# Last layer of a four-layer graph kernel: three rounded passes in place of full float32 products

## The reference, cut to what matters

```python
def _L3_gnn_ref(base_features, neighbor_mask, parent_child_mask, Wq, ..., alpha, gamma):
    x = base_features                      # 8192 x 256
    Q = x @ Wq + bq                        # 256 -> 128
    K = x @ Wk + bk
    V = x @ Wv + bv
    scores = einsum(Q, K) * scale + parent_child_mask * alpha, masked by neighbor_mask
    attn_out = einsum(softmax(scores), V)  # 64 x 64 per graph
    refined = attn_out @ Wo + bo + x       # 128 -> 256
    child_sum = einsum('nm,bmd->bnd', parent_child_mask, refined)
    ...
```

## Time and profile before

| | |
|---|---|
| median of 3 runs | 2340.16 us (2339.61 to 2341.25) |
| the profiled execution: its own time | 2342.6 us |
| its span, first to last instruction | 2340.7 us |
| PE busy | 2172.1 us, 93% of the span |
| DVE, ACT, POOL busy | 1391.9, 1206.5, 480.1 us |
| mean granted TensorE clock | 0.981 of full speed |

### The profile page before, as it was taken

One profiled execution on the slowest core, in us unless ns is written; L12 is line 12 of the kernel. 1 busy time (PEld: TensorE's weight loads), 2 busy tenths in 40 slices (PEclk: granted clock), 3 DMA queues, 4 the chain that ended last, 5 costly groups with the idle time before them and its releaser, 6 DMA issues. The chain is left out here.

```text
span 2340.7 us, 39332 instructions
## 1 busy us (share of the span) xinstructions
PE 2172.1 (93%) x14671; PEld 1939.7 (83%) x14671; DVE 1391.9 (59%) x2733; ACT 1206.5 (52%) x2295; POOL 480.1 (21%) x905
## 2 busy tenths in 40 slices
PE   5999999999969989999999999999998897979997
PEld 3888888888859988888888889988887897968886
DVE  3788778877855645443334433444433787857776
ACT  1453455345523347644444434444433566958887
POOL 3344334433430000000000000000000221016665
PEclk9999999999979999999999999999999898989999
DMA  2110111011122101000000000000000331012221
GB/s 97 33 55 18 40 49 54 18 40 49 37 82 63 54 30 36 1 18 1 1 1 19 19 1 1 1 1 1 1 1 18 107 109 54 0 32 64 72 72 50
DMA packets 76397, 81.77 MB, mean 35 GB/s; under 512 B 6545, under 2 KB 74001, under 8 KB 75409
## 3 DMA queue, kind: packets, MB, share of 16 engines
q1 hardware_dynamic: 76304, 80.51, 10.9%
HBM read 55.33 MB, written 25.17 MB: 34 GB/s over the span
## 5 line engine op out<-in xcount | busy, mean ns | idle before, releaser
L298 PE MATMUL ps<-R 128*128 128x256 f32 (+3 forms) x8520 | 1490.9, 335 | 38.2 <-DVE R L1506 14.2
L298 PEld LDWEIGHTS ps<-R 128*128 128x128 f32 x8520 | 1326.6, 190 | 183.2 <-DVE R L767 14.8
L1200 ACT ACTIVATE late_half<-ps,lstm_bias 128x512 f32<-128x512 f32 (+2 forms) x460 | 283.0, 669 | 383.0 <-PE ps L298 382.9
L340 POOL TENSOR_TENSOR ln_veps<-ln_mv,eps_tile 128x2 f32<-128x2 f32 x128 | 28.4, 222 | 1283.0 <-DVE ln_mv L323 1283.0
L829 PE MATMUL ps<-H 128*128 128x256 f32 x1024 | 237.6, 381 | 3.0 <-ACT H L750 1.7
L829 PEld LDWEIGHTS ps<-H 128*128 128x128 f32 x1024 | 189.0, 191 | 26.1 <-ACT H L750 1.9
L1235 DVE TENSOR_TENSOR late_half<-late_half 128x1024 f32<-128x1024 f32 (+2 forms) x32 | 37.6, 1175 | 186.8 <-ACT late_half L1200 186.8
L1197 ACT ACTIVATE late_half<-late_half 128x1024 f32<-128x1024 f32 (+2 forms) x66 | 68.1, 1031 | 124.4 <-DVE late_half L1240 78.4
L1237 DVE TENSOR_TENSOR late_half<-late_half 128x1024 f32<-128x1024 f32 (+2 forms) x32 | 37.6, 1175 | 132.6 <-ACT late_half L1200 132.6
L366 DVE SCALAR_TENSOR_TENSOR H<-H,ln_rstd 128x256 f32<-128x256 f32 x192 | 106.5, 596 | 6.7 <-POOL ln_rstd L333 3.2
L319 DVE BATCH_NORM_STATS2 ln_stats<-H 128x6 f32<-128x256 f32 x256 | 95.9, 416 | 5.3 <-POOL H L711 2.0
(11 more groups left out here) (208 smaller groups left out, 2860.6 us busy)
## 6 DMA issues: line engine op xcount, KB each, us to landing
H<-in_x SPq DMA_DIRECT2D x64, 256.0 KB, 4.1
residual<-H SPq DMA_DIRECT2D x32, 256.0 KB, 2.2
H<-residual SPq DMA_DIRECT2D x32, 256.0 KB, 2.9
arena<-residual SPq DMA_DIRECT2D x32, 256.0 KB, 2.7
residual<-arena SPq DMA_DIRECT2D x32, 256.0 KB, 2.2
H_state<-residual SPq DMA_DIRECT2D x32, 256.0 KB, 2.7
out<-H_state SPq DMA_DIRECT2D x32, 256.0 KB, 2.2
arena<-in_wih SPq DMA_DIRECT2D x4, 1024.0 KB, 5.0
```

What stands on the lines that cost most here:

```text
L298: mm = pe.matmul(out, lhsT(a), rhs(b), start=start and n == 0, stop=stop and n == len(PASSES) - 1)
L1200: ins = act.activation(into[q][:, m, 0:x.cols], gate_ps(q, m, x.cols), ACT.Tanh if q == TANH_G else ACT.Sigmoid, bias=lstm_bias[:, x.p - 1 ...
```

## The change

The query, key, value and output products of the last layer are issued through `exact_mm`, 12, 12 and 6 rounded passes in place of 4, 4 and 2 float32 products. Their inputs are split in two parts: ACT writes the rounded part where it wrote the copy (slots 3 and 10), and DVE, in two new slots 3 and 10, writes the rest. The weights are split once by GpSimd, during the third layer's second product. The ticks of the plan are set anew: PE's slots 4 to 12, ACT's 4 to 13, DVE's 6 to 12, POOL's 11 and 12 and SP's 13 move by one or two; the period and the leads stay.

```diff
         @block.gpsimd
         def _(pool):
+            pool.wait_ge(l3_loaded, 5 * 16)
+            for n, (split, w) in enumerate(splits3):
+                pool.tensor_scalar(split[:, 0], w, 1.0, None, ALU.mult).then_inc(w3_hi, 1)
+                pool.wait_ge(w3_hi, n + 1)
+                pool.tensor_tensor(split[:, 1], w, raw(split[:, 0]), ALU.subtract)
...
     plan4 = dict(
         period=34, lead=(0, 8, 17, 26),
-        pe={1: 19, 3: 28, 4: 30, 5: 32, 6: 35, 9: 42, 10: 44, 11: 46, 12: 48},
-        act={0: 8, 2: 27, 3: 29, 4: 34, 5: 38, 7: 38, 9: 43, 10: 45, 11: 48, 13: 57},
-        dve={1: 23, 6: 35, 8: 42, 11: 47, 12: 51},
-        pool={1: 23, 3: 28, 11: 48, 12: 51},
-        sp={10: 33, 13: 57})
+        pe={1: 19, 3: 28, 4: 31, 5: 33, 6: 36, 9: 43, 10: 45, 11: 48, 12: 50},
+        act={0: 8, 2: 27, 3: 29, 4: 35, 5: 39, 7: 39, 9: 44, 10: 46, 11: 50, 13: 59},
+        dve={1: 23, 3: 30, 6: 36, 8: 43, 10: 47, 11: 49, 12: 53},
+        pool={1: 23, 3: 28, 11: 50, 12: 53},
+        sp={10: 33, 13: 59})
...
-                    act.activation(xT3_f[s], feature_major(s, 1), ACT.Copy).then_inc(xT3_ready[s], 1)
+                    act.activation(xT3_r[s][:, 0], feature_major(s, 1), ACT.Copy).then_inc(xT3_hi[s], 1)
...
-                    act.activation(atT3[s], token_major(s, 1, P), ACT.Identity, bias=bv3_col[:, 0:1])\
-                       .then_inc(o3T_ready[s], 1)
+                    act.activation(oT3_r[s][:, 0], token_major(s, 1, P), ACT.Identity, bias=bv3_col[:, 0:1])\
+                       .then_inc(o3T_hi[s], 1)
...
+                if slot == 3:
+                    dve.wait_ge(xT3_hi[s], turn + 1)
+                    dve.tensor_tensor(xT3_r[s][:, 1], feature_major(s, 1), raw(xT3_r[s][:, 0]), ALU.subtract)\
+                       .then_inc(xT3_ready[s], 1)
+                if slot == 10:
+                    dve.wait_ge(o3T_hi[s], turn + 1)
+                    dve.scalar_tensor_tensor(out=oT3_r[s][:, 1], in0=token_major(s, 1, P), scalar=bv3_col[:, 0:1],
+                                             in1=raw(oT3_r[s][:, 0]), op0=ALU.add, op1=ALU.subtract)\
+                       .then_inc(o3T_ready[s], 1)
...
-            pe.wait_ge(l3_loaded, 5 * 16)
...
-                            mm = pe.matmul(feature_major(s, 0)[:, m, :], w[:, k, :], xT3_f[s][:, k, :],
-                                           start=(k == 0), stop=(k == KD - 1))
+                            mm = exact_mm(pe, feature_major(s, 0)[:, m, :], lambda q: w[:, q, k, :],
+                                          lambda q: xT3_r[s][:, q, k, :], k == 0, k == KD - 1)
...
-                            mm = pe.matmul(token_major(s, 1, ATT3)[:, n, :], xT3_f[s][:, k, n * P:(n + 1) * P],
-                                           Wv3[:, k, :], start=(k == 0), stop=(k == KD - 1))
+                            mm = exact_mm(pe, token_major(s, 1, ATT3)[:, n, :],
+                                          lambda q: xT3_r[s][:, q, k, n * P:(n + 1) * P],
+                                          lambda q: Wv3_r[:, q, k, :], k == 0, k == KD - 1)
...
-                        mm = pe.matmul(token_major(s, 0)[:, n, :], atT3[s][:, n, :], Wo3[:], start=True, stop=True)
+                        mm = exact_mm(pe, token_major(s, 0)[:, n, :], lambda q: oT3_r[s][:, q, n, :],
+                                      lambda q: Wo3_r[:, q, :], True, True)
```

More of the change, by code:

```diff
@@ L1457, in build_program @@
     bn2_var, bn2_pow, bn_steps2 = psem("bn2_var"), psem("bn2_pow"), psem("bn_steps2")
+    w3_hi = psem("w3_hi")
+    w3r = region(R[:, 4 * 2 * GATES * D:])
+    Wq3_r, Wk3_r, Wv3_r = (w3r(2, KD, ATT3) for _ in range(3))
+    Wo3_r = w3r(2, D)
+    splits3 = ((Wq3_r, Wq3), (Wk3_r, Wk3), (Wv3_r, Wv3), (Wo3_r, Wo3))
     plan3 = dict(
@@ L1546, in build_program @@
     x3_t, x3b_t, xr_t, y3_t = ([tiles_of(v) for v in b] for b in (x3, x3b, xr, xT3))
-    xT3_f = [blocks_of(v) for v in xT3]
+    r3 = region(R[:, 0:4 * 2 * GATES * D])
+    xT3_r = [r3(2, KD, GROUP) for _ in S]
+    oT3_r = [r3(2, TILES, P) for _ in S]
     (xr_loaded, hn_ready, h9_turned, var9, rstd9, x3_ready, x3b_ready, x3_turned, xT3_ready, qk3_done, qk3_ready,
@@ L1556, in build_program @@
     var9b, rstd9b = sems("l3_var_b"), sems("l3_rstd_b")
+    xT3_hi, o3T_hi = sems("l3_xT_hi"), sems("l3_oT_hi")
     plan4 = dict(
         period=34, lead=(0, 8, 17, 26),
-        pe={1: 19, 3: 28, 4: 30, 5: 32, 6: 35, 9: 42, 10: 44, 11: 46, 12: 48},
-        act={0: 8, 2: 27, 3: 29, 4: 34, 5: 38, 7: 38, 9: 43, 10: 45, 11: 48, 13: 57},
-        dve={1: 23, 6: 35, 8: 42, 11: 47, 12: 51},
-        pool={1: 23, 3: 28, 11: 48, 12: 51},
-        sp={10: 33, 13: 57})
+        pe={1: 19, 3: 28, 4: 31, 5: 33, 6: 36, 9: 43, 10: 45, 11: 48, 12: 50},
[3 more added lines that the diff above has]
+        sp={10: 33, 13: 59})
     with nc.Block() as block:
@@ L1713, in stage @@
                     pe.wait_ge(xT3_ready[s], turn + 1)
-                    for m, w in enumerate((Wq3, Wk3)):
+                    for m, w in enumerate((Wq3_r, Wk3_r)):
                         for k in range(KD):
-                            mm = pe.matmul(feature_major(s, 0)[:, m, :], w[:, k, :], xT3_f[s][:, k, :],
-                                           start=(k == 0), stop=(k == KD - 1))
+                            mm = exact_mm(pe, feature_major(s, 0)[:, m, :], lambda q: w[:, q, k, :],
+                                          lambda q: xT3_r[s][:, q, k, :], k == 0, k == KD - 1)
                     mm.then_inc(qk3_done[s], 1)
```

## The result

The changed kernel takes 2412.62 us (2410.72 to 2415.43, 4 runs) against 2339.89 (2339.42 to 2341.25, 4 runs): ratio 1.0311, 95% interval 1.0293 to 1.0329. It is 72.7 us slower; predicted were 72. The profiled execution took 2410.72 us, its span is 2408.2.

What follows compares the result with a forecast made beforehand. PE bounds the last layer before the change; afterwards a ring of waits was expected to. 2342.6 + 71 (ring) + 1 (weights) = 2414.6, with the profiled execution 2.4 above the median: 2412 us, range 2355 to 2436.

Steps and rivals of the forecast that it cites:

- PE's work: Last layer's products on PE: gains of 0.43 us against a loss of 0.45, +0.02 us a group, nothing.
- The narrow pass: Rounded 128-column pass of the value product, slot 5: 0.112 us taken, bounds 0.06 and 0.224.
- The rule on fast weight loads: Skill's rule for 128 non-FP32 weights: would put the value product towards its lower bound; the trace speaks against it.
- DVE: Two new split operations a group, slots 3 and 10: 1.0 us on top of 5.2, under 7.35, not full.
- The ring: Last layer's lists: new order closes a loop of waits, 10.5 + 9.3 + 18.5 = 38.3 us a round against 29.4; +71 us; chance 0.70.
- the sum along the lists: Method: follow the last layer's waits through the engines' lists and add durations; 38.3 us a round.
- Slot 5 outside the ring: Value product's price does not enter the last layer's time until PE's own sum passes 9.6 us a group.
- GpSimd: Weight split in the third layer's second product: eight operations, 5.1 us; cost taken as 1 us between 0 and 5.
- The clock: PE's granted clock in the last layer: stays at 1.00, the full 2.4 GHz.
- rival D: Last layer dearer: narrow pass at 0.224, 2422, or three rounds at half clock, 8.8 us each, 2438; chance 0.08.

Runs made afterwards that it cites:

- the ring cut: The changed kernel with three ticks one or two lower (DVE's slots 11 and 12, GpSimd's slot 11), same work; 2403.31 us, ratio 1.0274.
- the other places: The kernel before, its work unchanged to the instruction, with other leads and ticks; 2334.83 us, ratio 0.9974.

## Why the prediction was right

**PE's work.** Right. The narrow pass, which no row of before showed, takes what the weight load allows. Seven of the twelve passes of 128 columns of row 2205.05 above, by themselves:

```profile
2205.52 0.95 PE L298 MATMUL ps<-R 128*128 128x128 f32 x7
```

(0.95 - 0.28) / 6 = 0.112 us each; I took 0.112, between 0.06 and 0.224. The twelve take 1.48 until the next slot starts and not 1.34, as the first gap is longer. So the query, key and output products gain about what the value product loses. PE's busy time in the whole span grows by 9 us, but that does not measure the new passes: with the places alone, and the products of before, it is 2183.6 us, 11.5 above before.

**The rule on fast weight loads** (the Trainium skill, "TensorE: Matmul & The Clock Gate", Weight-path perf modes) would have put the narrow pass towards 0.06, if the rounded type counts as other than FP32. The trace does not show that: these passes follow each other by 0.112 us, as the float32 products of 128 columns did before, and like the rounded loads 0.11 apart of the earlier trace rows.

**DVE.** Slot 3 at 0.68 and slot 10 at 0.47 (0.68 and 0.45 taken). Not full, as said: 65% busy.

**The ring.** Right to 0.1 us in each of its three parts, and shown to be the cause: places without work +43.6, work without the new places +17.4, both 72.7. The two do not add up to 72.7, and the sum along the lists gives this too: +41, +20 and, for both, +72. At the new places the splits stand in the ring and cost 29 us, at the old ones 17. Slot 5 outside the ring was shown by leaving out two thirds of it: 38.30 us a round at the full clock.

**GpSimd.** Sized at 1 us between 0 and 5; 1.1 in the traces, not to be told from nothing in the times. Its eight operations were put at 5.1 us and took 9.7; that the delay stayed small fits their start 2.4 us ahead of DVE's first split. How it comes about is under the last heading.

**The clock.** Wrong: the forecast had it stay at 1.00, and only rival D let it fall. It did fall in the kernel after, behind an idle time of 1.88 us ahead of slot 11. That stretch, then a round without and the round with it:

```profile
2257.00:2262.00 5.00, 4.17 (x21) 3.75 (x22) 4.47 (x14) 1.86 (x5) 4.10 (x10) 0.74 0.00 0
...
2190.67:2228.98 38.31, 28.89 (x217) 26.19 (x217) 25.07 (x69) 25.95 (x61) 20.09 (x41) 1.00 0.18 55
2228.98:2267.27 38.29, 30.08 (x216) 27.39 (x216) 25.06 (x69) 25.96 (x61) 20.08 (x41) 0.96 0.17 55
```

Both rounds take 38.3 us, so the clock is no part of the loss here: from 2259 to 2263 us PE was in slots 4, 12 and 5, for which the ring does not wait at that point. Rival D's price, 8.8 us for a round at half clock, was for ring terms that ran at the full one. In the version with the ring cut such a stretch costs 1.3 us a round, and with one value pass one round lost 1.8.

**What was luck.** The sum of 2412 against 2412.6 is closer than the method: the same way of summing missed by 1 to 4 us in four versions, and by 9 and 7 in the ring cut and in the other places. That the falling clock met nothing that the ring waits for was not foreseen either.

## What to carry to other kernels

Where every engine works through a written list, a change of places is a change of its own: find for each wait what stands ahead of the awaited operation on its engine, follow that back until it closes, and add it up. Judge the new work at the old places first; here that separates 17 us from 73. A product in three passes of rounded parts is shorter on PE only where the moving side is wide (256 columns: 0.36 against 0.43 us; 128 columns: 0.34 against 0.22), and it can pay only if the split is not on the way to it. No run here gained by it in the last layer.

## What the runs showed of the hardware

GpSimd and VectorE held each other up while the weights were split. DVE of the kernel before, where GpSimd does nothing at that time, and then of the kernel with the weights split alone:

```profile
1978.32 0.69 DVE L1504 TENSOR_SCALAR R<-arena 128x1024 fp32r<-128x1024 f32 x1 [4.21 <-ACT arena L1481]
1979.05 1.23 DVE L1506 TENSOR_TENSOR R<-arena,R 128x1024 fp32r<-128x1024 f32 x1
```


```profile
1974.71 0.69 DVE L1514 TENSOR_SCALAR R<-arena 128x1024 fp32r<-128x1024 f32 x1 [4.22 <-ACT arena L1491]
1975.44 1.63 DVE L1516 TENSOR_TENSOR R<-arena,R 128x1024 fp32r<-128x1024 f32 x1
...
1979.05 1.22 DVE L1514 TENSOR_SCALAR R<-arena 128x1024 fp32r<-128x1024 f32 x1
```

The same copy takes 0.69 us alone and up to 1.22 beside GpSimd, the subtraction up to 1.63 in place of 1.23. GpSimd in the same kernel; its first two operations ran while DVE did nothing:

```profile
1972.30 0.87 POOL L1475 TENSOR_SCALAR R<-arena 128x256 fp32r<-128x256 f32 x1 [2.46 <-SPq L1469]
1973.25 0.72 POOL L1477 TENSOR_TENSOR R<-arena,R 128x256 fp32r<-128x256 f32 x1
...
1974.88 1.11 POOL L1477 TENSOR_TENSOR R<-arena,R 128x256 fp32r<-128x256 f32 x1
1975.96 2.16 POOL L1475 TENSOR_SCALAR R<-arena 128x256 fp32r<-128x256 f32 x1
```

Its eight operations took 9.7 us. Four times 0.87 and 0.72 would be 6.4, so some 3 us are from DVE; the 5.1 of the prediction, half of a 512-column operation each, was too low even for GpSimd alone. The Trainium skill ("SBUF — State Buffer", SBUF: two separate sides) calls the pair of ports exclusive: the one that comes second waits. The trace agrees in that both sides got longer only while the other worked, and in that DVE's copy of 1974.71, which began first, kept its 0.69 us while GpSimd's subtraction of 1974.88 took 1.11. That the second always waits for the whole of the other's instruction, these rows do not show.
